# The last stage of a transformer-block kernel: sorting products of two row groups in turn, a hand-written order for the last batch, and copies that read with strides

## The reference, cut to what matters

```python
def _L1_ffn_ref(x, Wc, bc, W1, b1, W2, b2):
    grouped = x.reshape(b, s // g, g, d)                       # groups of 32 tokens, 64 of them
    logits = jnp.einsum('bntd,des->bntes', grouped, Wc) + bc + tie
    perm = (logits == jnp.max(logits, axis=-3, keepdims=True)) # one token of 32, for each of 128 (e, s)
    permuted = jnp.einsum('bntd,bntes->bnesd', grouped, perm)
    inner = jax.nn.relu(jnp.einsum('bnesd,esdf->bnesf', permuted, W1) + b1)
    result_permuted = jnp.einsum('bnesf,esdf->bnesd', inner, W2) + b2
    return jnp.einsum('bnesd,bntes->bntd', result_permuted, perm)
x = x + cross_attention(layernorm(x), ctx_1024, ...)           # third layer
x = x + _L1_ffn_ref(layernorm(x), ...)                         # last layer
```

## Time and profile before

| | us |
|---|---|
| Median of 3 runs (lowest, highest) | 926.01 (925.89, 927.42) |
| The profiled execution | 924.24 |
| Its span in the profile | 922.5 |
| Mean clock granted to PE, share of full speed | 0.878 |
| PE, DVE, ACT, POOL busy | 715.2, 528.3, 344.3, 240.2 |
| First sorting product to first "e1" product | 803.7 to 848.6 |
| "e1" | 848.6 to 864.0 |
| "e2" | 864.0 to 893.5 |
| Turning back and combining | 893.5 to 922.5 |

### The profile page before, as it was taken

One profiled execution on the slowest core, in us unless ns is written; L12 is line 12 of the kernel. 1 busy time (PEld: TensorE's weight loads), 2 busy tenths in 40 slices (PEclk: granted clock), 3 DMA queues, 4 the chain that ended last, 5 costly groups with the idle time before them and its releaser, 6 DMA issues.

```text
span 922.5 us, 15737 instructions
## 1 busy us (share of the span) xinstructions
PE 715.2 (78%) x5815; PEld 539.4 (58%) x5815; DVE 528.3 (57%) x1283; ACT 344.3 (37%) x627; POOL 240.2 (26%) x234
## 2 busy tenths in 40 slices
PE   2657888878988888730999999964677769896898
PEld 2444656555655654420898899953544546575775
DVE  3547577887888786341112222224658888564585
ACT  1324454445546544500323222203044444543323
POOL 1513243333343322222102211005334441212000
PEclk9769898999999998855999999997598888865999
DMA  4969355865466573337556486503845432071002
GB/s 152 122 81 195 60 100 75 118 95 80 76 136 71 84 161 116 128 115 149 176 178 199 140 237 172 166 26 59 102 80 78 85 68 48 14 292 60 36 3 90
DMA packets 59848, 101.94 MB, mean 111 GB/s; under 512 B 7715, under 2 KB 50147, under 8 KB 54613
## 3 DMA queue, kind: packets, MB, share of 16 engines
q1 hardware_dynamic: 57357, 95.75, 47.5%
q0 software_dynamic: 2416, 5.19, 2.8%
HBM read 55.30 MB, written 7.28 MB: 68 GB/s over the span
## 4 chain that ended last, share of the span: by engine, by line
PE 48%; DVE 24%; DMA 8%; issue 6%; ACT 6%; SPq 4%; POOL 4%; ACTq 0%; DVEq 0%; POOLq 0%
PE PS L792 8%; PE U L803 8%; PE MB L635 7%; PE MB L730 4%; DVE nma L1152 4%; PE U L708 4%; PE PS L690 3%; DVE R L1356 3%; SPq L1566 2%; PE MB L667 2%; DMA La<-Uba 2%; DMA QKa<-mTa 2%; PE MB L882 2%; PE PS L847 2%; PE MB L651 1%
## 5 line engine op out<-in xcount | busy, mean ns | idle before, releaser
L1152 DVE TENSOR_REDUCE nma<-MB 128x2 f32<-128x512 f32 (+1 forms) x192 | 123.1, 670 | 32.7 <-PE MB L667 32.2
L970 ACT ACTIVATE Pa<-PS 128x1024 f32<-128x1024 f32 (+1 forms) x96 | 97.9, 1024 | 59.2 <-PE PS L690 57.9
L667 PE MATMUL MB<-QKa 99*128 99x120 bf16 (+1 forms) x512 | 73.6, 258 | 30.8 <-DVE nma L1152 15.8
L792 PE MATMUL PS<-mzT,mw 128*128 128x128 f32 x736 | 87.5, 278 | 1.8 <-ACT mzT L992 1.8
L803 PE MATMUL U<-mw,mdT 128*128 x368 | 83.5, 380 | 4.8 <-ACT mdT L1002 2.4
L792 PEld LDWEIGHTS PS<-mzT,mw 128*128 128x128 f32 x736 | 85.4, 194 | 2.7 <-issue 2.3
L1312 DVE TENSOR_TENSOR yt<-U,mb 128x256 f32<-128x256 f32 x23 | 9.8, 425 | 120.9 <-PE U L803 120.9
L667 PEld LDWEIGHTS MB<-QKa 99*128 99x128 bf16 x512 | 38.9, 104 | 64.2 <-DVE nma L1152 28.8
L803 PEld LDWEIGHTS U<-mw,mdT 128*128 128x128 f32 x368 | 68.2, 190 | 13.8 <-issue 5.5
L1400 POOL TENSOR_TENSOR mv<-mv,vec 128x2 f32<-128x2 f32 (+1 forms) x40 | 31.1, 777 | 140.5 <-DVE mv L1103 93.3
L690 PE MATMUL PS<-QKa 101*128 101x256 bf16 (+1 forms) x384 | 61.6, 285 | 3.1 <-DMA QKa<-mTa 3.1
(11 more groups left out here) (198 smaller groups left out, 1356.8 us busy)
## 6 DMA issues: line engine op xcount, KB each, us to landing
mw<-in_mw SPq DMA_DIRECT2D x31, 1024.0 KB, 6.0
QKa<-spa SPq DMA_DIRECT2D x144, 128.0 KB, 5.0
Qb<-spb SPq DMA_DIRECT2D x48, 128.0 KB, 4.4
Oa<-Uba SPq DMA_DIRECT2D x16, 256.0 KB, 3.6
v<-in_v SPq DMA_DIRECT2D x1, 4096.0 KB, 13.8
v<-in_v SPq DMA_DIRECT2D x4, 1024.0 KB, 11.9
W<-in_W SPq DMA_DIRECT2D x3, 1280.0 KB, 6.7
yb<-yt SPq DMA_DIRECT2D x23, 128.0 KB, 1.7
```

Source lines behind the costliest of these rows:

```text
L667: i = e.matmul(b[:, keys * j:keys * j + keys], Q[0:99, h0 + j, 128 * qt:128 * qt + 128], K[0:99, h0 + j, 0:keys], start=True, stop=True)
L792: i = e.matmul(ps[:, 128 * f:128 * f + 128], w[:, k, 128 * f:128 * f + 128], zz[:, k, :], start=k == 0, stop=k == 1)
L970: e.activation(p[0:keys, :], ps[0:keys, :], ACT.Exp, scale=0.25).then_inc(sems["exp"], 1)
L1152: e.tensor_reduce(A.nm[qt][:, h0:h0 + heads], b[:, 0:heads * keys].rearrange("p (h s) -> p h s", h=heads), AX.X, ALU.max, negate=True).the ...
```

## The change

It touches only what comes after the last attention product, and the shapes in which three kinds of instructions go through memory.

1. The order after ("pv", 23, 3) no longer comes from the planner but from a list, last_order(). ("gp", 0, 0) with its copies moves behind ("pv", 23, 3) and ("p2", 22). The steps of batch 23 (p0 to fp) stand among fewer sorts: two sorts stand between the end of "pv" and "p0", where there were five.
2. copy_on() decides who copies: half c = 0 of each pair goes to ACT, half c = 1 to DVE, but for k = 0 of even batches ACT copies both. A pair is free when both counts are reached.
3. "sort" on PE: row groups 0 and 2 are multiplied in turn, product by product, then 1 and 3. Groups 0 and 1 now write bank 0, 2 and 3 bank 1; the second two wait for the first two.
4. The copies into G read PSUM with strides (1 KB, then 512 bytes) and write pairs of neighbouring values. The addition into R reads PSUM with a stride of 256 bytes and writes four neighbouring values.
5. The weights ("wt") also wait for the DMA into Ob of batch 23; the last two blocks of v2 also wait for the end of "e1".

```diff
-T_GATHER = (-0.0149, 0.25)
+def last_order():
+    out = [("p2", 22), gp(0, 0), gc(0, 0, 0), gc(0, 0, 1), ("fm", 21), gp(0, 1), gc(0, 1, 0), gc(0, 1, 1), ("wt",),
+           ("na", 22, 3), ("fp", 21), ("p0", 23), ("ps", 23), ("nb", 22, 3), gp(1, 0), gc(1, 0, 0), gp(1, 1), ("p1", 23),
+           ("ft", 22), gc(1, 0, 1), gc(1, 1, 0), ("p2", 23), gc(1, 1, 1), gp(2, 0), gc(2, 0, 0), ("na", 23, 3), gc(2, 0, 1),
+           gp(2, 1), gc(2, 1, 0), ("fw", 22), ("nb", 23, 3), gc(2, 1, 1), gp(3, 0), gc(3, 0, 0), ("ft", 23), ("fm", 22),
+           gc(3, 0, 1), ("fw", 23), gp(3, 1), gc(3, 1, 0), ("fp", 22), gc(3, 1, 1), ("fm", 23), gp(4, 0), gc(4, 0, 0),
+           gc(4, 0, 1), ("fp", 23), gp(4, 1), gc(4, 1, 0), gc(4, 1, 1)]
+    for b in range(5, NB):
+        for k in range(2):
+            out += [gp(b, k), gc(b, k, 0), gc(b, k, 1)]
+    return out
+def copy_on(b, k, c):
+    return "a" if c == 0 or (k == 0 and b % 2 == 0) else "b"
...
-            for r in range(4):
-                if r >= 2:
-                    g.wait_ge("gp", done + r - 1)
+            for pair_of in ((0, 2), (1, 3)):
+                if pair_of[0]:
+                    g.wait_ge("gp", done + 2)
                 for tt in range(2):
                     for part in range(3):
                         z = z2[:, t, :] if part == 2 else z01[:, t, part, :]
-                        i = e.matmul(ps[:, 512 * (r % 2) + 256 * (r // 2) + 128 * tt:][:, 0:128],
+                        for r in pair_of:
+                            i = e.matmul(ps[:, 512 * (r // 2) + 256 * (r % 2) + 128 * tt:][:, 0:128],
...
-                dst = G[:, k, :, 8 * b:8 * b + 8].rearrange("p s (t a c) -> p c a t s", a=2, c=2)
-                src = pair("gp", b, k)[:, :].rearrange("p (c a t s) -> p c a t s", c=2, a=2, t=2)
+                dst = G[:, k, :, 8 * b:8 * b + 8].rearrange("p s (t c a) -> p c s t a", c=2, a=2)[:, c]
+                src = pair("gp", b, k)[:, :].rearrange("p (c a t s) -> p c s t a", c=2, a=2, t=2)[:, c]
...
-            e.tensor_tensor(R[:, :, :, s:s + 4].rearrange("p k n s -> p k s n"), bank("e2", b, q)[:, :].rearrange("p (k s n) -> p k s n", k=2, s=4),
-                            over(c2[:, :, s:s + 4], 64, 3), ALU.add).then_inc(sems["down"], 1)
+            e.tensor_tensor(R[:, :, :, s:s + 4], bank("e2", b, q)[:, :].rearrange("p (k s n) -> p k n s", k=2, s=4),
+                            over(c2[:, :, s:s + 4], 64, 2), ALU.add).then_inc(sems["down"], 1)
...
         def set_weights():
             g.wait_ge("pv", len(UNIT))
+            g.wait_ge("d_o1", 16 * 12)
...
             g.wait_ge("sorted_b", copies("b", 7, 1))
+            g.wait_ge("e1", 4)
             for b in (1, 2):
                 e.dma_start(v2[:, 8 * b:8 * b + 8, :], D["v2"][:, 8 * b:8 * b + 8, :]).then_inc(sems[f"d_v2{b}"], 16)
```

More of the change, by code:

```diff
@@ L162, in order @@
     others.append(([-0.2, 0.6], [[("sl",)], [("wc",)]]))
[L163 to L167, removed]
+    steps = pipeline(16, 8, others)
+    end = steps.index(("pv", 23, 3)) + 1
+    last = last_order()
+    assert sorted(steps[end:]) == sorted(s for s in last if s[0] not in ("gp", "gc"))
+    out += steps[:end] + last
     out += [("ex",)] + [("e1", b) for b in range(4)]
@@ L194, in count, with copies @@
     return NO[what][key]
+def copies(engine, b, k):
+    return sum(copy_on(*s[1:]) == engine for s in STEPS if s[0] == "gc" and s[1:3] <= (b, k))
 class Ring:
@@ L253, in score_users @@
         elif what == "gp":
-            yield s, (("sorted_a" if key[1] == 0 else "sorted_b", 2 * key[0] + 2),)
+            yield s, tuple((f"sorted_{w}", copies(w, key[0], key[1])) for w in "ab")
         elif what == "cm":
@@ L846, in sort @@
                         z = z2[:, t, :] if part == 2 else z01[:, t, part, :]
-                        i = e.matmul(ps[:, 512 * (r % 2) + 256 * (r // 2) + 128 * tt:][:, 0:128],
-                                     z[32 * r:32 * r + 32, 128 * k:128 * k + 128], pT[32 * r:32 * r + 32, t, :],
-                                     start=part == 0, stop=part == 2)
-                i.then_inc(sems["gp"], 1)
+                        for r in pair_of:
+                            i = e.matmul(ps[:, 512 * (r // 2) + 256 * (r % 2) + 128 * tt:][:, 0:128],
+                                         z[32 * r:32 * r + 32, 128 * k:128 * k + 128], pT[32 * r:32 * r + 32, t, :],
+                                         start=part == 0, stop=part == 2)
+                            if (tt, part) == (1, 2):
+                                i.then_inc(sems["gp"], 1)
         def sets_up(b):
@@ L854, in sets_up @@
             g.wait_ge("d_v1", 16)
-            g.wait_ge("sorted_a", 16)
-            g.wait_ge("sorted_b", 16)
+            g.wait_ge("sorted_a", copies("a", 7, 1))
+            g.wait_ge("sorted_b", copies("b", 7, 1))
             g.free(BANKS.free["e1", b])
```

16 lines of the change are left out of this document (10 added, 6 removed).

## The result

| | us |
|---|---|
| Before, median of 4 runs (lowest, highest) | 925.95 (923.51, 927.42) |
| Changed, median of 4 runs (lowest, highest) | 916.09 (915.55, 917.15) |
| Ratio (95% interval) | 0.9898 (0.9874, 0.9921) |
| The profiled execution, its span | 915.83, 914.0 |

The kernel became faster by 9.9 us; the forecast was 7.2, and 918.8 us lies 2.7 above the measured 916.1, well within its range of 914.0 to 923.6. In the changed kernel the lines of the old one stand some 30 further down: sorts are L879, their copies L1063 (ACT) and L1374 (DVE), "e1" L895, "e2" L905 with the addition L1389.

The account below looks back on a forecast made before the run. PE's work was taken to set the sorting stage, instruction supply "e1", DVE's additions "e2". Gains 4.0 + 0.8 + 1.7 + 0.7 = 7.2 us, off the median of 926.01, gave 918.8; range 914.0 to 923.6, forecast's chance 0.54.

Parts of the forecast that it names:

- The sorting stage: Sorts and copies before "e1": new list ends 4.0 us sooner by layings of steps on engines, plus 0.8 for L1329.
- L1329: DVE instruction at batch 23, 1.18 us beside a POOL instruction against 0.41: falling behind POOL's work gains 0.8 us.
- Order: Sorting stage: batch 23's L730 starts near 814.3, not 824.3; the layings of old and new lists differ by 4.0 us.
- From there PE has work without end, and its work sets the stage: Sorting stage from batch 23's L730 on: PE work totals 23.0 us, plus 2.5 us of waits; copies end at 842.3.
- the changed order does not do what it says: Rival, sorting stage: PE is bound by its own work in either order; 2 us less gain, 920.8; no chance given.
- The clock, 0.16: Rival, sorting stage: with fewer pauses PE's clock stays up; 4 us more gain, 914.8; chance 0.16.
- wrong would be the forecast, too, if the granted clock is above 0.50 from 817 on: Sign against the forecast, in the sorting stage: PE's granted clock above 0.50 from 817 on.
- Reads: Copies into G and addition into R: strided PSUM reads taken as free, a second copy about 0.55 us, not 0.85.
- Both rivals that charged them: Strided PSUM reads cost like strided writes (921.9, chance 0.17) or twice a plain copy (930.4, chance 0.13).
- "e1": v2 loads slow the instruction supply, a 2.44 us first wait; moving them behind "e1" gains 1.7 us, bounds 0 and 2.4.
- "e2": DVE's additions pace it at 0.88 us, PE nearly as long; a cheap addition gains 0.7 us and leaves PE pacing.
- In turn: Sorts on PE: alternating row groups gains 0.13 us a sort, bounds 0 and 0.27; 0.5 of the 4.0.

## Why the prediction was right, and where it was not

**The sorting stage: 4.8 forecast, 8.2 measured.** The stage's end was laid at 842.3, 39.6 us behind the mark; it came at 37.7. The laying of the old list ended at 846.3, 43.6 behind the mark, and the trace had 45.9, so the 3.4 us missed are 1.9 of the new list and 2.3 of the old, less the 0.8 added for L1329 (the gain was 4.0 + 1.9 + 2.3 = 8.2). The layings are given by their ends alone, so which of their waits were wrong can't be read off.

Much of the gain was there, but under the wrong name. The paragraph called "Order" subtracted a laying of the new list from one of the old, and the new one carried the new order, the split over two engines and cheap copies all at once. The runs separate them as far as they go: the order cost 1.4 with the old copies and at the same clock, and was worth 0.5 in the new surroundings (some 2 by the estimate at an equal clock), the split 3.7, the reads 2.5 to 5.3. These do not add up to 8.2, since what one edit is worth depends on the others and on the clock.

"From there PE has work without end, and its work sets the stage" is the sentence that failed: eleven sorts were priced at 1.26 us each, from a row of two sorts in a row, which is exactly as many as there are free pairs. From the third on the cycle of a pair decides. In the changed kernel that mistake is small, since split and cheap copies bring the cycle to 1.36 us, and it works the other way: it would have made the new list longer. It is the order's 4 us that hang on it, as the kernel before with the new order alone shows, with 1.93 a sort. What made the new list shorter than laid is the clock (see below).

The first reading, that PE is "busy nearly throughout", holds only up to 827.6: from 831.0 to 848.5 PE was busy for 11.95 of 17.50 us. The rival "the changed order does not do what it says" had the right thought (the order is worth little) but not this reason.

**The clock, 0.16, came true in part.** The sentence "wrong would be the forecast, too, if the granted clock is above 0.50 from 817 on" is met: 0.82 over 817.5 to 828, 6.7 us at the upper level. The prediction had laid just that, the new list "with 7 us of it at 839.3", 3.0 us sooner than its forecast, and priced the rival at 4. With it the new list would have ended 36.6 us behind the mark, and it ended 1.1 later. So the clock more than accounts for what the new list gained over its laying. The clock is also a part of why the reads are worth 5.3 and not 2.5 us in the new surroundings. Counted from the start of L760 of batch 23 to the run of seven sorts, the same steps take 16.0 us in the changed kernel and 18.6 with the old shapes (820.51 to 839.09), where the clock fell sooner:

```profile
820.50:828.00 7.50, 6.50 (x61) 4.68 (x60) 3.83 (x10) 4.89 (x6) 2.26 (x3) 0.73 0.93 395
828.00:852.00 24.00, 19.97 (x254) 13.16 (x253) 14.70 (x18) 16.42 (x19) 3.10 (x4) 0.50 0.15 59
```

That is 2.6 of the 5.3, by the estimate above 1.8 of it the clock's; longer waits for copies are in it too (0.83 us for 0.41 ahead of the second sort), and the two were not separated. The run of seven and its last copies are 2.2 more (10.8 and 13.0), at 0.50 in both kernels, by the cycle with copies of 1.31 us; 0.5 lies ahead of L760. What decides that the clock stays up or falls I can't say from these runs; it repeated in all four profiles with this sorting code, whose stages lie between 37.6 and 37.7 us.

**L1329, 0.8.** It takes 0.41 us in the changed kernel at batch 23, as said, and 1.10 in the changed kernel with the old order. But in its place the two Yz instructions of that batch now run beside POOL, 1.50 us in the chain at 824.60, where batch 22's two took 0.74 at 815.82. The step moved the collision, it did not remove it.

**Reads.** Free, as chosen: 691 ns for the addition, and copies at 708 and 658. Both rivals that charged them are out. The Trainium skill's rule that non-contiguous patterns in PSUM's lines of 8 bytes are slow (PSUM — Partial Sum Buffer, Specifications) is stated for products, and it doesn't carry over to DVE and ACT: they read four bytes at a time 256 bytes or 1 KB apart at full speed here. What the old shapes paid for is the write: the rows show 1025 - 691 = 334 ns, with steps of 512 bytes. The Trainium skill's Vector Engine (DVE) Microarchitecture Reference (5.2 Measured stream behaviour on trn2) gives 1.71 instead of 1.054 ns a column when the destination hops 4 KiB at each element, from which I estimate 0.34 us more for 512 columns. The same table has 2.50 for a destination stepping 24 words, from which it would be 0.74; the rows here, with steps between the two, agree with the first.

**"e1": 1.7 forecast, 3.2 measured.** The mechanism stands, and its size is right within what could be told apart: 1.0 to 1.9. What was missed, 1.3 us or more, I put down to the clock and to the number of instructions at hand, untested. The forecast had not counted on either, so this part is luck.

**"e2": 0.7 forecast, 0.9 measured.** PE needs 27.89 us and DVE waits for it, as said.

**In turn: 0.13 a sort forecast, 0.15 measured;** worth 1.2 to 1.4 us of the tail in all, where 0.5 were taken, though only 0.5 in the sorting stage when laid alone.

**The sum.** 12.3 us of stages against 7.2. That the medians differ by only 9.9, and so close to the forecast, owes 2.4 us to the drift ahead of the mark. That is luck: without it the time would have been some 913.7, below the range of 914.0 to 923.6.

## What to carry to other kernels

Price a step that fills and empties buffers by its cycle, filling plus emptying over the number of buffers, when that is more than the producer's pace, and not by the pace in a row that is no longer than there are buffers. When several edits are laid together, take them back one at a time before giving the gain a name, and look at the granted clock over the same stretch before comparing two of them. And if a transposing copy must have strides on one side, try them on the PSUM side.

## What the hardware showed beside that

- ACT and DVE read PSUM with a stride of 256 bytes or more at the price of a plain read (691 and 604 ns). Writing single values 8 bytes apart into SBUF is also free (686 ns on DVE, 604 on ACT in the kernel with the read strides alone), writing them 256 bytes apart costs a half more on DVE (1030) and three quarters more on ACT (1060). The Trainium skill's lines of 16 bytes, of which two hits are wanted (Advanced Engine Details and Errata, Memory Cachelines), fit both.
- When ACT and DVE start on the two halves of a pair at the same moment, each takes some 0.73 us; when DVE starts 0.07 us behind ACT, they take 0.61 and 0.68, as alone, though they overlap nearly as much. With the old shapes the same is 1.3 us against 1.04 and 1.01. So it is not the overlap alone that costs, and no run shows what else it is:

```profile
825.94 0.61 ACT L1063 ACTIVATE G<-PS 128x512 f32<-128x512 f32 x1 [0.59 <-PE PS L879]
826.01 0.68 DVE L1374 COPY G<-PS 128x512 f32<-128x512 f32 x1
...
835.27 0.73 ACT L1063 ACTIVATE G<-PS 128x512 f32<-128x512 f32 x1 [0.92 <-PE PS L879]
835.27 0.72 DVE L1374 COPY G<-PS 128x512 f32<-128x512 f32 x1 [2.62 <-PE PS L879]
```

- A shorter stage can hand its gain back through the clock: the old sorting step made sorting 1.1 us shorter, at a mean clock of 0.78, and "e1" with "e2" 2.2 to 2.5 longer.
